# Feed-forward in another order with its constants and statistics made ahead, and a third PSUM bank for rolled keys

## The reference

```
h = gelu(x @ w1a + mean(slots) @ w1b + b1);  logits = (h @ w2 + b2) / (|tau| + 0.1)      # 64 slots
alpha = softmax over the top 8 logits, zero elsewhere                                     # token x 64
si = (alpha^T x) / sum(alpha)                                                             # slot x 128
r, z = sigmoid of (si @ Wih + bih + S @ Whh + bhh);  n = tanh(i_n + r * h_n)
S' = (1 - z) * n + z * S;  q, k, v = S' @ wq + bq, ...;  y = S' + softmax(q k^T) v
out = alpha @ ((layernorm(y) * ln_g + ln_b) @ wvp + bvp) @ wo + bo
```

## Time and profile before

| | us |
|---|---|
| median of 3 runs | 945.12 (944.6 to 946.56) |
| the profiled execution | 945.51 |
| its span, first to last instruction | 943.7 |
| PE busy | 789.8 (84%) |
| DVE busy | 672.3 (71%) |
| ACT busy | 480.2 (51%) |
| POOL busy | 409.8 (43%) |
| mean granted TensorE clock | 0.922 of full |

### The profile page before, as it was taken

The page is one execution under the profiler, slowest core; times in us unless marked ns, Lnnn a source line. Parts: engine busy times, 40 slices in busy tenths (PEclk is TensorE's granted clock), DMA queues, the critical chain, the costliest instruction groups (busy, mean ns, idle before and its releaser), DMA issues.

```text
span 943.7 us, 25617 instructions
## 1 busy us (share of the span) xinstructions
PE 789.8 (84%) x10324; PEld 606.5 (64%) x10324; DVE 672.3 (71%) x1528; ACT 480.2 (51%) x849; POOL 409.8 (43%) x302
## 2 busy tenths in 40 slices
PE   1899999999999999999986876667888888839655
PEld 0688888888888888888875553534555555525435
DVE  3767667776677766677674776536999999966773
ACT  1678766787767777677752423013444433315220
POOL 1454444544445444454442100116888888751000
PEclk9999999999999999999996778768999999958786
DMA  6000000000000000000000000000221111120002
GB/s 274 1 3 1 0 0 0 0 0 0 0 0 0 0 0 0 0 0 0 1 1 2 0 1 1 1 0 1 23 24 22 22 22 22 20 27 1 1 1 89
DMA packets 71588, 13.25 MB, mean 14 GB/s; under 512 B 66432, under 2 KB 70528, under 8 KB 70912
## 3 DMA queue, kind: packets, MB, share of 16 engines
q1 hardware_dynamic: 71552, 12.76, 6.2%
HBM read 8.56 MB, written 4.19 MB: 14 GB/s over the span
## 4 chain that ended last, share of the span: by engine, by line
PE 63%; DVE 19%; ACT 8%; issue 5%; POOL 3%; DMA 1%; DVEq 0%; ACTq 0%; SPq 0%; POOLq 0%
PE PS L533 6%; PE PS L490 6%; PE PS L349 5%; PE PS L350 4%; PE PS L351 4%; PE PS L426 3%; PE PS L732 3%; DVE b_prod L843 3%; PE PS L722 3%; PE PS L526 2%; PE PS L512 2%; PE PS L724 2%; PE PS L1015 2%; DVE a_nm L607 2%; PE PS L497 2%
## 5 line engine op out<-in xcount | busy, mean ns | idle before, releaser
L640 POOL TENSOR_TENSOR a_pl<-a_p,a_ph 128x1024 f16<-128x1024 f32 (+1 forms) x128 | 210.7, 1646 | 256.3 <-ACT a_ph L562 256.3
L891 POOL TENSOR_TENSOR b_w<-b_v,b_e 128x2048 f32<-128x2048 f32 x32 | 137.8, 4307 | 13.9 <-ACT b_e L811 13.9
L559 ACT ACTIVATE a_p<-PS 128x1024 f32<-128x1024 f32 (+1 forms) x128 | 103.7, 810 | 74.8 <-PE PS L497 74.7
L607 DVE TENSOR_REDUCE a_nm<-PS 128x4 bf16<-128x512 f32 (+1 forms) x128 | 121.5, 949 | 0.0
L843 DVE TENSOR_TENSOR b_prod<-PS,b_qt 128x512 f32<-128x512 f32 x128 | 85.4, 682 | 26.3 <-PE PS L724 22.0
L562 ACT ACTIVATE a_ph<-PS 128x1024 f16<-128x1024 f32 (+1 forms) x128 | 103.1, 805 | 0.0
L552 ACT ACTIVATE a_qk_h<-PS 128x512 f16<-128x512 f32 x128 | 73.4, 604 | 57.1 <-PE PS L351 55.8
L372 POOL TENSOR_TENSOR veps<-mv,eps 128x2 f32<-128x2 f32 (+2 forms) x40 | 8.0, 201 | 190.4 <-DVE mv L1165 136.9
L596 DVE TENSOR_TENSOR a_qk_l<-PS,a_qk_h 128x512 f16<-128x512 f32 x128 | 87.0, 681 | 3.4 <-ACT a_qk_h L552 3.4
L512 PE MATMUL PS<-a_vh,a_ph 128*128 128x65 f16 x768 | 78.5, 196 | 0.3 <-issue 0.3
L514 PE MATMUL PS<-a_vl,a_ph 128*128 128x64 f16 x768 | 78.3, 194 | 0.0
(11 more groups left out here) (225 smaller groups left out, 2038.7 us busy)
## 6 DMA issues: line engine op xcount, KB each, us to landing
scratch_dram<-b_o SPq DMA_DIRECT2D x32, 64.0 KB, 3.6
b_y<-scratch_dram SPq DMA_DIRECT2D x16, 128.0 KB, 2.1
out_dram<-X SPq DMA_DIRECT2D x2, 1024.0 KB, 3.9
w_rest<-rest_dram SPq DMA_DIRECT2D x1, 1862.0 KB, 15.2
X<-x_dram SPq DMA_DIRECT2D x1, 1792.0 KB, 11.2
w_first<-first_dram SPq DMA_DIRECT2D x1, 1600.0 KB, 7.1
w_rolls<-rolls_dram SPq DMA_DIRECT2D x1, 544.0 KB, 15.8
X<-x_dram SPq DMA_DIRECT2D x1, 256.0 KB, 3.6
```

Of the source, the lines that this page charges most:

```text
L559: act.activation((a_p0, a_p1)[j][:, me, :, :, :].rearrange("p a h q -> p a (h q)"), TT[:, :, 0:512 - 256 * j], ACT.Exp, scale=EA ** -0.5)
L607: dve.tensor_reduce(a_nm[:, nx, j, :].rearrange("p (a h) -> p a h", a=2)[:, :, 0:2], MM[:, :, 0:256 * (j + 1)].rearrange("p a (h k) -> p a ...
L640: pool.tensor_tensor(*(n[:, g % 2, :, :, :].rearrange("p a h q -> p (a h q)") for n in (pl, p, ph)), ALU.subtract).then_inc(a_split, 1)
L891: pool.tensor_tensor(b_w8[:, j, :, :, :], rolled_values(par, j, 0, H), rolled_exps(par, j, 0, H), ALU.mult).then_inc(b_weighed, 1)
```

## The change

The plans, the norm and the constants:

```diff
@@ a_steps (last batch)
-        put(last and g == 2, ("ffn_stats", 0))
-        put(last and g == 3, ("ffn_apply", 0))
+        put(last and g == 2, ("ffn_stats", 0), ("ffn_rstd", 0))
+        put(last and g == 3, ("set", 0), ("ffn_apply", 0))
@@ b_steps (tail=True in the last batch only)
     put(True, "sumexp")
+    put(tail, ("ffn_stats", 0))
     put(one, ("roll", 5), ("dots", 0))
@@
-A_EPILOGUE = [("normal", 0, 0), ("turn", 0, 0), ("pv", 0, 0), ("pv", 0, 1), ("normal", 1, 0), ("turn", 1, 0),
-              ("project", 1, 0)]
+A_EPILOGUE = [("normal", 0, 0), ("turn", 0, 0), ("pv", 0, 0), ("pv", 0, 1), ("normal", 1, 0), ("set", 1, 1), ("turn", 1, 0),
+              ("ffn_stats", 1, 1), ("ffn_rstd", 1, 1), ("project", 1, 0)]
@@
-              ("project", 1, 0), ("finish", 1, 0), ("ffn_stats", 0, 0), ("add", 1, 0), ("ffn_apply", 0, 0), ("yt", 1, 0),
+              ("ffn_rstd", 0, 0), ("ffn_stats", 0, 1), ("ffn_rstd", 0, 1), ("project", 1, 0), ("finish", 1, 0),
+              ("add", 1, 0), ("ffn_apply", 0, 0), ("yt", 1, 0),
@@
-F_PLAN = [("stats", 1), ("hidden", 0), ("apply", 1), ("logits", 0), ("hidden", 1),
...
+F_PLAN = [("stats", 2), ("hidden", 0), ("apply", 1), ("apply", 2), ("logits", 0), ("hidden", 1), ("logits", 1),
+          ("topa", 0), ("topb", 0), ("topa", 1), ("expo", 0), ("expo", 1), ("alpha", 0), ("read", 0), ("topb", 1), ("slots", 0),
+          ("inputs", 0), ("wih", 0), ("alpha", 1), ("gates", 0), ("candidate", 0), ("read", 1), ("new", 0), ("slots", 1),
+          ("qkv", 0), ("inputs", 1), ("scores", 0), ("wih", 1), ("gates", 1), ("probs", 0), ("candidate", 1), ("attend", 0),
+          ("new", 1), ("qkv", 1), ("values", 0), ("scores", 1), ("out", 0), ("probs", 1), ("attend", 1), ("add", 0),
+          ("values", 1), ("out", 1), ("add", 1)]
+PIECES = [(0, CT), (CT, CT - 4), (NT - 4, 4)]
```

```diff
@@ f_tensor
                 if kind == "hidden":
-                    pe.wait_ge(f["normed"], k)
                     if c == 0:
+                        pe.wait_ge(f["normed"], len(PIECES) * rep + 1)
+                        if rep == 0:
+                            pe.wait_ge(a_exped, 2 * GA * NB)
+                        else:
+                            pe.wait_ge(b_multiplied, ROLLS * NB)
+                            pe.wait_ge(b_raised, 2 * NB)
+                            pe.wait_ge(b_exped, NB)
+                    else:
+                        pe.wait_ge(f["normed"], len(PIECES) * rep + 2)
                         pe.wait_ge((a_added, b_added)[rep], NB)
@@
+                elif kind == "wih":
+                    pe.wait_ge(f["alt_ev"], k)
+                    for n in range(2):
+                        pe.matmul(B[2 + n][:, :].rearrange("p (b s) -> p b s", s=NS), ident[:, :],
+                                  gate_h[:, n:n + 1, :].to_broadcast([128, CB, NS]), start=True, stop=False)
                     pe.wait_ge(f["sit"], k)
-                    pe.wait_ge(f["alt_ev"], k)
                     for n in range(3):
-                        ins = pe.matmul(B[1 + n][:, :], w["wih_t"][:, n * 128:(n + 1) * 128], v["sit"][:, :],
-                                        start=True, stop=True)
-                    ins.then_inc(f["gi_mm"], 1)
+                        pe.matmul((B[2], B[3], B[1])[n][:, :], w["wih_t"][:, n * 128:(n + 1) * 128], v["sit"][:, :],
+                                  start=n == 2, stop=True).then_inc(f["gi_mm"], 1)
                 elif kind == "qkv":
+                    pe.wait_ge(f["gates_tanh"], 2 * k)
+                    pe.matmul(B[2][:, :].rearrange("p (a d) -> p a d", a=PAIRS), ones[0:1, :],
+                              w["bv"].unsqueeze(1).to_broadcast([1, PAIRS, D]), start=True, stop=False, skip_group_check=True)
@@ attend
                     ins.then_inc(f["y_mm"], 1)
-                elif kind == "ynorm":
-                    pe.wait_ge(f["y"], k)
+                    pe.matmul(B[2][:, :], ident[:, :], v["sn"][:, :], start=True, stop=False, skip_group_check=True)
                     for p in range(PAIRS):
-                        ins = pe.transpose(B[2][:, p * 128:(p + 1) * 128], v["y"][:, p, :], ident[:, :])
+                        sl = slice(p * 128, (p + 1) * 128)
+                        ins = pe.matmul(B[2][:, sl], v["v"][:, p, :], v["pt"][:, sl], start=False, stop=p == PAIRS - 1,
+                                        skip_group_check=True)
                     ins.then_inc(f["yt_mm"], 1)
@@ f_scalar, gates and qkv
-                    act.activation(v["r"][:, :], v["r"][:, :], ACT.Tanh, scale=0.5)
-                    act.activation(v["zg"][:, :], v["zg"][:, :], ACT.Tanh, scale=0.5).then_inc(f["gates_tanh"], 1)
+                    for n, dst in ((0, v["r"]), (1, v["zg"])):
+                        act.wait_ge(f["gi_mm"], 3 * (k - 1) + n + 1)
+                        act.activation(dst[:, :], B[2 + n][:, :], ACT.Tanh, scale=0.5).then_inc(f["gates_tanh"], 1)
@@
+                    act.wait_ge(f["v_mm"], k)
+                    act.activation(v["v"][:, :, :].rearrange("p a d -> p (a d)"), B[2][:, :], ACT.Copy).then_inc(f["v"], 1)
@@ f_vector, alpha
+                    link(dve.tensor_reduce(f_sum[:, :], v["e"][:, :, NS:NS + TOPK], X_AXIS, ALU.add))
+                    dve.reciprocal(f_sum[:, :], f_sum[:, :])
...
-                    link(dve.tensor_reduce(f_sum[:, :], v["al"][:, :, :], X_AXIS, ALU.add))
-                    link(dve.reciprocal(f_sum[:, :], f_sum[:, :]))
@@ f_vector: the steps "gates" and "ynorm" go, v's bias too; values
-                    dve.tensor_tensor(v["so"][:, :, :], pairs(B[3][:, :]), crow[:, :].unsqueeze(1)
-                                      .to_broadcast([128, PAIRS, D]), ALU.add).then_inc(f["so"], 1)
-                elif kind == "out":
+                        ins = dve.scalar_tensor_tensor(v["so"][:, p, :], pairs(B[3][:, :])[:, p, :], rstd[:, n:n + 1],
+                                                       crow[:, :], ALU.mult, ALU.add)
+                    ins.then_inc(f["so"], 1)
+                elif kind == "add":
```

`top` is split into `topa` (maxima and subtraction, with the eight maxima less the first put behind the 64 values of each token) and `topb` (match_replace); the exponentials are the step `expo`, one buffer per chunk. The first chunk's `hidden` uses banks 2 to 5, where it used 0 to 3. Attention B:

```diff
+        ROLLED, DOTS = PS[2:5], PS[5]
@@ b_tensor
-                    wait(pe, b_multiplied, m - 1)
+                    wait(pe, b_multiplied, m - 1 if j < 2 else m - 2)
                     for e in range(2):
-                        pe.matmul(T[j % 2][:, e * SEQ:(e + 1) * SEQ], w["roll"][:, 2 * j + e, :], b_kh[:, nx, :],
+                        pe.matmul(ROLLED[j % 3][:, e * SEQ:(e + 1) * SEQ], w["roll"][:, 2 * j + e, :], b_kh[:, nx, :],
@@ dots
-                    wait(pe, b_raised, 2 * b + j + 1)
+                    wait(pe, b_raised, 2 * (b + 1) + j)
-                            ins = pe.matmul(M[j][32 * n:32 * n + 32, 0:SEQ], w["heads"][:, e, :], b_prod[:, 4 * j + n, e, :],
+                            ins = pe.matmul(DOTS[32 * n:32 * n + 32, j * SEQ:(j + 1) * SEQ], w["heads"][:, e, :], b_prod[:, 4 * j + n, e, :],
```

More of the change, by code:

```diff
@@ L97, in a_steps, with b_steps @@
         put(g == 1 and not first, ("project", 0))
-        put(last and g == 2, ("ffn_stats", 0))
-        put(last and g == 3, ("ffn_apply", 0))
+        put(last and g == 2, ("ffn_stats", 0), ("ffn_rstd", 0))
+        put(last and g == 3, ("set", 0), ("ffn_apply", 0))
     return steps
-def b_steps(par, former=True, before=True, third=True, ahead=True, ahead2=True):
+def b_steps(par, former=True, before=True, third=True, ahead=True, ahead2=True, tail=False):
     one, two = ahead, ahead2
@@ L167 @@
           (b_steps(0) + b_steps(1), 2, NB // 2 - 3),
-          (b_steps(0, ahead2=False) + b_steps(1, ahead=False, ahead2=False), NB // 2 - 1, None),
+          (b_steps(0, ahead2=False) + b_steps(1, ahead=False, ahead2=False, tail=True), NB // 2 - 1, None),
           (B_EPILOGUE, NB // 2, None)]
-F_PLAN = [("stats", 1), ("hidden", 0), ("apply", 1), ("logits", 0), ("hidden", 1),
-          ("logits", 1), ("top", 0), ("alpha", 0), ("read", 0), ("top", 1), ("slots", 0), ("inputs", 0), ("alpha", 1),
-          ("read", 1), ("gates", 0), ("slots", 1), ("inputs", 1)]
-LATER = ["gates", "candidate", "new", "qkv", "scores", "probs", "attend", "ynorm", "values", "out"]
-F_PLAN.append(("candidate", 0))
-for n in range(2, len(LATER) + 2):
-    F_PLAN += [(LATER[m], c) for m, c in ((n, 0), (n - 2, 1)) if m < len(LATER)]
+F_PLAN = [("stats", 2), ("hidden", 0), ("apply", 1), ("apply", 2), ("logits", 0), ("hidden", 1), ("logits", 1),
[5 more added lines that the diff above has]
+PIECES = [(0, CT), (CT, CT - 4), (NT - 4, 4)]
 class Fill:
```

214 lines of the change are left out of this document (111 added, 103 removed).

## The result

The changed kernel takes 902.25 us, the median of 3 runs (900.19 to 903.35), against 945.12 before: a ratio of 0.954, 95% interval 0.9508 to 0.9572. The forecast was 916.5 us with a range of 908 to 929. The direction was right; the gain, 42.9 us, is half again the 29 forecast. The profiled execution is the one of 902.25 us, its span 900.4. Beside the experiments further down, the kernel before took 946.1 to 946.5 us, 1 us more than here; the kernel after was not run beside them, so a difference of under about 1.5 us to its 902.25 says nothing.

The account below looks back on a forecast made before the run. Attention A was taken as PE-bound, B as DVE-bound, the tails as chains of short steps with no engine full. Terms -4.4 -0.5 -20 -2.4 -0.7 -1.0 = -29.0 took 945.5 to 916.5 us, range 908 to 929.

Parts of the forecast that it names:

- Attention B: DVE's 14 listed waits for rolls go with a third bank, -2.4 us; B's first 35 us give -0.7.
- Hidden 0's clock: First feed-forward: PE enters hidden 0 without the pause that put it at half clock, -0.5 us (0 to -2).
- The start: Constants moved ahead start the first hidden 0 earlier, -4.4 us (-1.8 to -5.5); statistics ahead start the second earlier, -1.0.
- The forecast's other reason: At A's end: the 16 applies, moved to where POOL is idle, take 4.2 us instead of 6.82.
- The tails: From last logit matmul to last addition in each feed-forward: four edits sum to 10.9 us, taken as -10 each.
- The order laid out by hand: The tail's new steps placed on four engines at their profiled durations: last addition 55.4 us behind the last logit.
- the rival of a PE-bound tail: The tails gain little because PE becomes their bound: 67 us each, 936.5 us in all; chance 0.17.
- (a): Tail: the weights' sum is taken from 8 exponentials instead of 64 selected ones, -1.0 us per chunk.
- (b): Tail: gate biases enter through PE and ACT reads PSUM, net -2.6 us per chunk.
- (c): Tail: the norm of y is applied after the value product, net -2.5 us per chunk.
- (d): Tail: DVE takes chunk 1's maxima before chunk 0's alpha, +1.3 us, once.
- The rivals: PE-bound tail 936.5 us, chance 0.17; slower 971, 0.02; starts gain nothing 922.5, 0.09; change not doing what it says 945, 0.02.

Follow-up runs that it names:

- e2: The kernel before with only attention B's part of the change (three banks for rolled keys, one for dot products): 935.2 us, ratio 0.9889 to before.
- e1: The kernel after with the rolled keys back in two banks, the single dots bank kept: 911.7 us.
- e3: The kernel after with two banks for rolled keys and each roll made of the high half of k alone: 903.7 us.
- e9: The kernel after with the sum of the weights taken over the 64 selected ones again: 904.4 us.
- e16: The kernel after with both gate tanhs waiting for all three input products instead of each for its own: 907.9 us.
- e8: The kernel after with the gate biases added on DVE again instead of by products on PE: 901.6 us.
- e7: The kernel after with the norm of y back ahead of the value product: 922.8 us.
- e14: The kernel before with only y's transpose made by PE and the norm of y behind the value product: 936.9 us, ratio 0.9904.
- e6: The kernel after with alpha of chunk 0 ahead of chunk 1's maxima and exponential, slots 0 ahead of chunk 1's match_replace: 897.0 us, ratio 0.9459.
- e15: The kernel after with the feed-forward's steps in the order of before, all operations as after: 924.6 us.
- e5: The kernel after with both parts of the constants put back behind attention A: 906.0 us.
- e11: The kernel after with alpha 0 early, gate biases on DVE, constants' second part earlier and sixteen unread PE products at A's end: 897.6 us.

## Why the prediction was right and wrong

**Attention B: wrong, and the largest miss.** The step that failed reads "DVE waits once per batch for the roll", 2.4 us, and "a third bank ... more than the 0.17 that DVE waits". It took the listed waits for all waits. The third bank is worth 11.3 us in the kernel before (e2) and 9.5 in the kernel after (e1), and PE's rows and e3 show the mechanism: a loop of 1.39 us for two products that need 1.20. The sign stood in the earlier trace rows: DVE was busy 164.6 of 172, so it was idle for 7.4 us, three times the 2.4 listed. The rest was read as work, when up to 0.09 us of a product's slot was a wait. The list after has no wait for rolls in the 14 batches, as forecast, but a batch went from 12.25 us to 11.53, not to 12.1.

**Hidden 0's clock: the mechanism right, the size wrong.** The term was -0.5 (bounds 0 to -2) and the trace shows -4.3. The clock before came back at 530 only and was at half again from 536.7 to 540; after, it is full from 520 to 541. Over the profiles it is -1.5 to -4.3. The forecast counted hidden 0's own slow start and not that the clock would also stay up behind it.

**The start: right in the one trace, with a term missed.** -3.2 against -4.4; most of the difference, 0.9 us, is the constants' second part, which cost 1.2 and was put at 0.3, at full clock. That the clock at 499 to 504 can be half, which costs 2.5 us more and leaves 0.3 of the gain, was not among the bounds (-1.8 to -5.5). In the second feed-forward the start gained 1.5 against 1.0.

The forecast's other reason held as well: the applies took 4.1 us with POOL idle. But the 4.19 us at 809.65 are the same although POOL's power ran beside them for 2.29 us. The Trainium skill, "SBUF — State Buffer", "SBUF: two separate sides", has the shared port locked for a whole instruction. The 6.82 us beside the subtractions agree with it: one apply took 2.14 us, one 1.17 and the other fourteen 0.33 to 0.34 each, as many long ones as subtractions. The 4.19 beside the power do not agree, and the power was not held up either (2.27 us at A's end, where DVE is idle).

**The tails: the sum right, its terms wrong.** The order laid out by hand gave 55.4 us, and the tail took 55.4 and 55.6, with PE at 0.91 and 0.88 of its clock; the rival of a PE-bound tail falls. That was no luck: the layout holds step by step, with new 0 done 21.8 us behind the last logit (22.4 by hand), probabilities 0 at 28.1 (28.4), values 0 at 40.6 (40.8), probabilities 1 at 43.4 (43.5) and values 1 at 51.6 (51.8). The terms beside it were right only as a sum. Each was sized on the chain of before and multiplied by two, "since both chunks stand in one chain now". The runs show:

| term | forecast per tail | undone in the new order |
|---|---|---|
| (a) sum of 8 | -2.0 | 0.3 to 0.7 (e9) |
| (b) gates | -5.2 | hand-off 0.6 and 3.0 (e16); bias on PE a loss of 1.0 to 1.6 (e8) |
| (c) norm of y | -5.0 | 9 (e7); 3 to 5 in the old order (e14) |
| (d) maxima first | +1.3 | a loss of 2.7 to 2.9 (e6) |
| the rest of the order | none | 7 with (d)'s loss in it (e15) |

In the old order all operations together give 4 us of the 11. The order was the largest part, and the forecast had a negative term for it. It was in the layout by hand, and nowhere in the sum; that the two agreed (10.9 and 11.2) was taken for a confirmation, and was chance.

**The rivals** all fell, and the range with its lower end at 908 had no room for a gain in B beyond the listed waits, since 0 to -2.4 was taken as its whole bound. (The lower bounds it names add up to 909.0, not 908: 916.5 - 6 - 1.5.) The second feed-forward's stretch from hidden 0 to the last logit, for which no term stood, is 20.1 to 24.5 us over the profiles: the 1.0 us more goes with the clock, 0.78 where it was 0.82.

**The smaller points** held: gather 1 released by POOL, hidden 0 right behind the last projection in both stages, the single dots bank free (e1 has it, and its batches take the 12.25 us of before).

## What to carry to other kernels

Measure a busy engine by the distance between starts of equal operations, and compare it with a place where the same operation runs unhindered: in a ring of two buffers a wait shorter than the overlap of two records shows as work, and one a little longer may be in no list. Compare the listed waits with the idle time that the window leaves. When steps of two chunks share engines in order, the sum of single savings says little; lay the whole order out step by step, and test an order as one edit and the operations as another. Put what can be done early (the constants, a product without use) into the pause that comes before a long stretch of PE, since here the pause was paid for again in the clock of what followed. And look where in two traces a difference stands before giving it to an edit: in e5, e11 and e16 a good part of the total stood where the edit was not.

## What the hardware showed that was not expected

- Unlinked operations of DVE on 128x512 f32 have records of 0.69 us and start 0.60 apart; under a ring's wait they start 0.60 to 0.83 apart (0.70 to 0.72 on the mean) with the same record.
- The same steps of the same code found PE at 2.4 GHz in some executions and at 1.2 in others (the constants' products, six f32 ones in 0.88 us in the kernel after and 1.54 in e1). e6's runs fell into two pairs 10 us apart, 891.7 and 891.9, 902.0 and 903.6, with mean clocks of 0.961 and 0.942 to 0.944. Attention A's last subtractions start anywhere from 498.5 to 500.7. A median of a few runs of such a kernel is uncertain by that much, and gains under 5 us above are only as good as their stretch of the trace.
- The clock fell without idle time too: in e6, e7, e8 and e15 it was half for nearly 7 us, from the end of logits 0 into hidden 1. In e6 PE was busy 4.00 of the 4.00 us before the fall and 7.00 of 7.00 in it (530 to 541). In the tails, where the prediction expected activity to keep the clock up, it did rise with fewer pauses (0.76 to 0.91); it does not explain this place. What decides it there is left open.
- DVE's sixteen applies were not slower beside POOL's power (4.19 us at 809.65), and were beside its subtractions (6.82; the same 6.82 in e2, e5 and e14).
